# Two of fourteen large block products written out plainly, and the planner of sums, loads and tile places rewritten around them

## The reference, cut to what matters

```python
# x: (32, 128, 2048), all float32
def _L0(x, weight, bias, A, B, scale, id7):        # weight: (2048, 2048), A: (8, 16, 2048)
    base  = einsum('bsi,oi->bso', x, weight) + bias
    low   = einsum('bsi,bri->bsr', x, A[id7])
    delta = einsum('bsr,bor->bso', low, B[id7])
    return base + scale[id7][:, None, None] * delta
def _L1(x, weight, id14):                           # weight: (16, 2048, 2048)
    return einsum('bij,bkj->bik', x, weight[id14])
x = x + _L0(x, ...)
x = x + _L1(x, ...)
```

## Time and profile before

| | |
|---|---|
| median of three runs | 2754.98 us |
| the profiled execution | 2748.32 us |
| its span | 2746.5 us |
| mean granted TensorE clock | 0.971 |
| PE busy | 94% |
| DVE busy | 80% |
| ACT busy | 51% |
| POOL busy | 28% |

### The profile page before, as it was taken

How to read it: one execution, slowest core, us unless ns; L and a number is a source line. 1 busy time by engine, 2 the same in 40 slices (tenths; PEclk the granted TensorE clock), 3 DMA queues, 4 the chain that set the end, 5 groups by cost and what they waited for, 6 DMA issues and landing times.

```text
span 2746.5 us, 35355 instructions
## 1 busy us (share of the span) xinstructions
PE 2590.8 (94%) x12154; PEld 2128.2 (77%) x12154; DVE 2197.3 (80%) x1990; ACT 1389.4 (51%) x1486; POOL 779.1 (28%) x646
## 2 busy tenths in 40 slices
PE   7988789999998979997999999999999999999999
PEld 5767677878876767786888888888878878878887
DVE  7778679998885879987788887777877867877865
ACT  3324233334433323335666675666666756656665
POOL 4234334433333344411032131320320401302402
PEclk9999899999999989998999999999999999999999
DMA  5886796664389656976768768778699998998996
GB/s 218 320 290 204 195 245 174 197 202 155 111 265 264 170 140 162 291 251 239 274 228 301 250 225 298 252 261 275 243 343 342 326 355 337 321 346 306 310 320 232
DMA packets 218323, 702.97 MB, mean 256 GB/s; under 512 B 23936, under 2 KB 32288, under 8 KB 218144
## 3 DMA queue, kind: packets, MB, share of 16 engines
q1 hardware_dynamic: 201728, 640.94, 64.8%
q0 software_dynamic: 16128, 58.73, 10.9%
q10 hardware_dynamic: 288, 1.05, 0.1%
HBM read 675.45 MB, written 92.27 MB: 280 GB/s over the span
## 4 chain that ended last, share of the span: by engine, by line
PE 67%; DMA 13%; DVE 10%; issue 5%; POOL 2%; SPq 2%; ACT 1%; DVEq 0%; POOLq 0%; ACTq 0%
PE acc L1203 15%; PE acc L1204 15%; PE acc L1205 15%; PE acc L1120 7%; PE acc L1121 7%; PE acc L1122 7%; DMA wb<-w 5%; DMA xb<-x 4%; DVE tx L1075 2%; DVE ws L1075 2%; DMA xb<-x_sums 2%; DMA x_sums<-xb 1%; DVE acc L1064 1%; PE acc L1159 1%; DVE xb L980 1%
## 5 line engine op out<-in xcount | busy, mean ns | idle before, releaser
L1075 DVE TENSOR_TENSOR ws<-wb,ws 128x1024 fp32r<-128x1024 f32 x964 | 1244.5, 1318 | 322.9 <-ACT ws L906 310.1
L906 ACT CAST ws<-wb 128x1024 fp32r<-128x1024 f32 x964 | 985.7, 1050 | 793.0 <-PE acc L1205 422.7
L1203 PE MATMUL acc<-ws,ops 128*128 128x512 f32 (+1 forms) x2048 | 804.9, 393 | 33.8 <-DVE lows L1018 18.6
L1204 PE MATMUL acc<-ws,ops 128*128 128x512 f32 (+1 forms) x2048 | 801.5, 391 | 0.0
L1205 PE MATMUL acc<-ws,ops 128*128 128x512 f32 (+1 forms) x2048 | 800.8, 391 | 0.0
L1120 PE MATMUL acc<-tx,ws 128*128 128x512 f32 x1568 | 629.2, 401 | 112.9 <-DVE tx L1075 99.6
L815 POOL TENSOR_TENSOR wb<-wb,eye_s 128x128 f32<-128x128 f32 x384 | 318.6, 860 | 1201.9 <-DMA wb<-w 1201.7
L1121 PE MATMUL acc<-tx,ws 128*128 128x512 f32 x1568 | 624.5, 398 | 0.0
L1122 PE MATMUL acc<-tx,ws 128*128 128x512 f32 x1568 | 623.1, 397 | 0.0
L906 ACT CAST tx<-xb 128x1024 fp32r<-128x1024 f32 x196 | 205.9, 1051 | 538.3 <-PE acc L1122 268.9
L1203 PEld LDWEIGHTS acc<-ws,ops 128*128 128x128 f32 x2048 | 387.2, 189 | 115.9 <-DVE lows L1018 20.0
(11 more groups left out here) (66 smaller groups left out, 1115.8 us busy)
## 6 DMA issues: line engine op xcount, KB each, us to landing
wb<-w SPq DMA_DIRECT2D x832, 512.0 KB, 8.6
xb<-x SPq DMA_DIRECT2D x78, 512.0 KB, 7.0
y<-acc SPq DMA_DIRECT2D x32, 1024.0 KB, 6.7
xb<-x POOLq DMA_DIRECT2D x64, 512.0 KB, 9.2
out<-ost SPq DMA_DIRECT2D x128, 256.0 KB, 7.4
xst<-xt SPq DMA_DIRECT2D x60, 512.0 KB, 7.2
ystage<-y SPq DMA_DIRECT2D x60, 512.0 KB, 11.2
wb<-w_sums SPq DMA_DIRECT2D x48, 512.0 KB, 8.5
```

The lines of the kernel that those rows point to most:

```text
L906: eng.copy(hi, src).then_inc(s_hi, 1)
L1075: eng.tensor_tensor(lo, src, hi, ALU.subtract).then_inc(s_lo, 1)
L1203: eng.matmul(dst, yh, wh, start=begin, stop=False)
L1204: eng.matmul(dst, yh, wl, start=False, stop=False)
```

## The change

1. Outer products 0 and 1 (PLAIN) are computed by the class `Eight`: eight steps, all from unsummed tiles, no inner sums. Pairs of steps add up in the same PSUM bank, so that only every second step is evicted, and a split x tile (T) serves two steps (`new_t`), so that four steps have T splits. The other twelve products keep the seven steps (`Seven`). The stage has 100 steps instead of 98.
2. The weight sums of n = 2 to 5 are all made in advance by POOL (m1 to m4, for each of 8 halves p): four loads, four sums, and four stores to w_sums for each p. DVE's 16 "made" sums and all 48 accumulating weight DMAs are gone. Loads for n = 2 to 5 come from w_sums alone.
3. Places of x tiles follow need: the role that the next product needs first (b11) takes the place that is left first (step 3), then b12 (4), b22 (5), b21 (6).
4. `beside` has a second wait where DVE evicts the named step: POOL's inner sum also waits for the DVE task that stands just before the eviction of that step. s4 now goes through `beside` too, and s4 and s3 are planned with both halves in one step (t_of(s0 + 2), t_of(s0 + 3)): their first halves 8 to 11 us later than before, their second halves within 3 us of where they were.
5. Keys of t3 and t2 move later (t3 from s0 - 2 to s0 - 1), the accumulating x DMAs from +9 to +10.5, the saves of x sums from +16 to +22 after their load's key.

```diff
+class Eight:
+
+    t = ("b11", "b21", "b11", "b21", "b12", "b22", "b12", "b22")
+    w = ("a11", "a12", "a21", "a22", "a11", "a12", "a21", "a22")
+    blk = (None, 0, None, 2, None, 1, None, 3)
+    new_t = (0, 1, 4, 5)
+    fresh = (0, 2, 4, 6)
...
+    x_need = ("b11", "b21", "b12", "b22")
+    x_done = (("b11", 0), ("b21", 1), ("b12", 4), ("b22", 5))
+    w_need = ("a11", "a12", "a21", "a22")
+    w_done = (("a11", 4), ("a12", 5), ("a21", 6), ("a22", 7))
...
+class Seven:
...
+    x_need = ("b11", "b12", "b22", "b21")
+    x_done = (("b11", 3), ("b12", 4), ("b22", 5), ("b21", 6))
+    w_need = ("a21", "a22", "a11", "a12")
+    w_done = (("a21", 3), ("a11", 4), ("a12", 5), ("a22", 6))
...
+PLAIN = (0, 1)
+FORM = [Eight if q in PLAIN else Seven for q in range(NG * K)]
+STEPS = [(q, i) for q in range(NG * K) for i in range(len(FORM[q].t))]
...
-    def made_key(d, p):
-        return (18.0 + 9.0 * p, 32.0 + 15.0 * p)[d]
+    def made_key(p):
+        return MADE_FROM + MADE_EVERY * p
...
+            key = t_of(s) + (24 * h - 48) * MM + (3.2 if FORM[q] is Seven and (i, h) == (4, 0) else 0.25)
...
+    for p in range(8):
+        for i in range(4):
+            loads.append((made_key(p) - 12.0 + 0.1 * i, "made", (p, i)))
+        for i, after in ((1, 3.0), (0, 6.0), (2, 9.0), (3, 12.0)):
+            loads.append((made_key(p) + after, "keep", (p, i)))
...
-        if n in W_ADDED:
-            for role in W_ROLE:
-                for h in range(2):
-                    adds.append((lo_key("W", s0 - K + W_FREE[role], h) + 9.0, "wacc", (q, role, h)))
-        for h in range(2):
-            adds.append((past(s0 - 2 + h, 0.3) if q else -8.5 + 4.0 * h, "s1", (q, h)))
-            adds.append((past(s0 + h, 0.3) if q else lo_key("W", 0, h) + 8.0, "s2", (q, h)))
-            adds.append((past(s0 + 1 + h, 3.0 if h == 0 else 2.9), "s4", (q, h)))
-            adds.append((past(s0 + 2 + h, 0.3), "s3", (q, h)))
...
+        if FORM[q] is Eight:
+            continue
+        for h in range(2):
+            adds.append((t_of(s0 - 2 + h) + 0.3, "s1", (q, h)))
+            adds.append((t_of(s0 + h) + 0.3, "s2", (q, h)))
+            adds.append((t_of(s0 + 2) + 0.3 + 2.5 * h, "s4", (q, h)))
+            adds.append((t_of(s0 + 3) + 0.3 + 2.5 * h, "s3", (q, h)))
+        for c in range(2):
+            sums.append((t_of(s0 - 1) + 6.0 + 0.1 * c, "t3", (q, c)))
+            sums.append((t_of(s0 - 1) + 8.3 if c == 0 else t_of(s0) + 6.5, "t2", (q, c)))
+            sums.append((t_of(s0) + 8.0 + 0.1 * c, "t4", (q, c)))
+            sums.append((t_of(s0 + 1) + 8.0 + 0.1 * c, "t1", (q, c)))
...
+    for p in range(8):
+        for i, kind in enumerate(("m1", "m2", "m3", "m4")):
+            adds.append((made_key(p) + 3.0 * i, kind, (p,)))
...
+        before_ev = {}
+        for n, (_, what, _, index) in enumerate(vector_tasks):
+            if what == "ev" and index[1] == 0 and n:
+                _, was, k, old = vector_tasks[n - 1]
+                if was == "lo":
+                    before_ev[index[0]] = (s_lo, k + 1)
+                elif was == "ev":
+                    before_ev[index[0]] = (s_ev, ev_no[old])
+                elif (was, *old) in sum_no:
+                    before_ev[index[0]] = (s_sum, sum_no[(was, *old)])
...
+                if p >= 2:
+                    made_kept(eng, p - 2, i)
+                    eng.wait_ge(s_pool, pool_no["m4", p - 2])
...
             def beside(eng, s):
 
-                if s >= 0:
-                    eng.wait_ge(s_mm, at["W", s, 3] + 1)
+                if s in before_ev:
+                    eng.wait_ge(*before_ev[s])
+                eng.wait_ge(s_mm, at["W", s, 3] + 1)
```

More of the change, by code:

```diff
@@ L58 @@
 HOME = {"Y": (0, 0), "Z": (0, 1), "X": (1, 0), "Q": (1, 1)}
[L59 to L73, removed]
@@ L74 @@
-WS = [slots_of(("a11", "a12", "a21", "a22"), W_NEXT, q) for q in range(NG * K)]
+MADE_OF = ((1, 0), (1, 1), (0, 0), (0, 1))
+MADE_AS = (2, 0, 1, 3)
+MADE_FROM = 10.0
+MADE_EVERY = 18.0
+class Eight:
[4 more added lines that the diff above has]
+    fresh = (0, 2, 4, 6)
+    turn = (0, 2, 4, 6)
+    first = (1, 3, 5, 7)
+    last = {0: 1, 2: 3, 1: 5, 3: 7}
+    x_need = ("b11", "b21", "b12", "b22")
+    x_done = (("b11", 0), ("b21", 1), ("b12", 4), ("b22", 5))
+    w_need = ("a11", "a12", "a21", "a22")
+    w_done = (("a11", 4), ("a12", 5), ("a21", 6), ("a22", 7))
@@ new lines @@
+class Seven:
+    t = ("b11", "b21", "b11", "b11", "b12", "b22", "b21")
+    w = ("a11", "a12", "a11", "a21", "a11", "a12", "a22")
+    blk = (0, 0, 1, 3, 3, 1, 2)
+    new_t = (0, 1, 2, 3, 4, 5, 6)
+    fresh = (0, 1, 3)
+    turn = (0, 1, 2, 3, 4, 5, 6)
+    first = (0, 2, 3, 6)
+    last = {0: 1, 1: 5, 3: 4, 2: 6}
+    x_need = ("b11", "b12", "b22", "b21")
+    x_done = (("b11", 3), ("b12", 4), ("b22", 5), ("b21", 6))
+    w_need = ("a21", "a22", "a11", "a12")
+    w_done = (("a21", 3), ("a11", 4), ("a12", 5), ("a22", 6))
@@ L208, in program @@
                 if q == 0:
-                    key = -30.0 + {"a11": 1.0, "a21": 4.5, "a22": 8.0, "a12": 14.0}[role] + 1.2 * h
+                    key = -30.0 + {"a11": 1.0, "a12": 4.0, "a21": 10.0, "a22": 13.0}[role] + 1.2 * h
                 else:
-                    key = lo_key("W", s0 - K + W_FREE[role], h) + 1.5
+                    key = lo_key("W", W_FREED[q][role][1], h) + 1.5
                 loads.append((key, "w", (q, role, h)))
[L213 to L217, removed]
+    for p in range(8):
[3 more added lines that the diff above has]
+            loads.append((made_key(p) + after, "keep", (p, i)))
     tile_no = [None] * NRAW
@@ L292, in program @@
     fast, slow = [], []
-    for s in range(NSTEP):
-        n, i = s // K % K, s % K
-        for ot in range(4):
-            (fast if n in (0, 2) and i in FIRST else slow).append((ev_key(s, ot), s, ot))
+    for s, (q, i) in enumerate(STEPS):
+        if evicts(s):
+            for ot in range(4):
+                (fast if q % K in (0, 2) and i in FORM[q].first else slow).append((ev_key(s, ot), s, ot))
     fast.sort()
@@ L996, in _ @@
                         eng.tensor_tensor(q, x, q, ALU.add).then_inc(s_sum, 1)
-                    continue
-                if what == "made":
-                    d, p = index
-                    made_loaded(eng, d, p)
-                    one, other = made_tile(d, p, 0), made_tile(d, p, 1)
-                    eng.tensor_tensor(other, one, other, ALU.subtract).then_inc(s_sum, 1)
                     continue
```

307 lines of the change are left out of this document (169 added, 138 removed).

## The result

The changed kernel took 2622.78 us (median of four runs, 2619.82 to 2624.97) against 2749.96 us for the kernel before on the same chip: a ratio of 0.9539, with a 95% interval of 0.9507 to 0.9570. That is 127 us, 4.6% faster. The forecast was 2650 us with a range of 2612 to 2702, so sign and range held, and the gain was 27 us more than forecast. A second set of runs of the same kernel gave 2623.42 us, ratio 0.9548 (0.9523 to 0.9574).

A forecast was written before the change was run, and what follows sets the result against it. First-stage stalls and slow matmuls, 163 us over 10.88 us steps, were the winnable bound. Start 12.0 + steps 1100.0 + residues 5, 16, 7, 15 + second stage 1504.6 + 1.8 around gave 2649, said as 2650 us; range 2612 to 2702.

The forecast's parts named there:

- the residues: Stalls forecast to remain over the step floor in the first stage: 5, 16, 7 and 15 us, bounds 5 to 118.
- three releasers: Behind DVE in the first stage: late x tiles, DVE's own load with POOL collisions, and b21, whose place is left last.
- Products 0 and 1: First two products, 46.9 us over the floor: eight steps leave 5 us, between 0 and 25, with DMA the doubtful cover.
- Rival A: DMA at mean rates bounds the first 186 us, delaying made sums and x loads: 20 to 25 us more, 2672; chance 0.13.
- Products 2, 3, 9 and 10: Stalls of 71.2 us: fewer accumulating DMAs and earlier b11 leave 16 us, between 0 and 40.
- I leave 4 us for each: In products 2, 3, 9 and 10, b21 is late next and its store holds t4: 16 us in all.
- Products 4, 11 and 12: Stalls of 22.7 us: POOL's new wait leaves 2 to 4 collisions with DVE instead of 8; 7 us remain.
- Products 6 and 13: Stalls of 22.5 us: only collisions go, b21's load is neither earlier nor lighter; 15 us remain, between 5 and 30.
- B: DVE and b21 stay the bound: products 4, 6, 11, 12, 13 keep their stalls, four more get 6 us: 2697; chance 0.17.
- E: No change: the wait shifts from b11 to b22, t3 stalls DVE in products 2, 3, 9, 10: 2728 or 2743; chance 0.03.
- D: Slower: POOL, DVE and ACT lock in a ring of waits, delaying each of 96 inner halves; 2804 at 1.6 us; chance 0.04.
- C: Nearly all first-stage stalls go, residues of 10 us in all: 2617 us; chance 0.08.

## Why the prediction was right, and where it was off

**The bound.** Right: nearly all of the gain is in the first stage, its steps cost 10.88 us, and stalls and slow matmuls went together. Its end was forecast near 1143 us and is at 1119.6. These 23.4 us, in the residues, are most of the error of 27; the rest is rounding, 1.2 us in the second stage and the 2.2 us between the profiled execution and the median. What the list of three releasers lacked is a fourth: DVE's t3 and t2 behind the stores of x sums, 47.7 us, with PE's 10.7 us at the end of product 2.

**Products 0 and 1.** I left 5 us, and 3.7 stand, all in product 0. The cover held, but closely: the DMA share from 90 us to the start of product 2 is over 1.

```profile
90.00:150.00 60.00, 60.00 (x266) 49.70 (x265) 38.53 (x22) 21.09 (x23) 41.93 (x19) 1.00 1.03 377
150.00:190.00 40.00, 40.00 (x179) 33.11 (x178) 27.00 (x20) 8.48 (x9) 19.40 (x14) 1.00 1.04 362
```

The count of 175 to 191 us of transfers in 184 was about right: in the two products the DMA engines were busy for some 177 us and moved 64.5 MB, where I had counted 67. Rival A did not come: the last of the made sums' stores was issued at 176.5 us, 13 us before product 2, and nothing on PE stood for them. The rate here is 362 to 377 GB/s for a hundred microseconds, and so under the 410 GB/s of 10 us, a short row that was no rate to plan with. The Trainium skill gives about 358 as the limit (DMA: Bandwidth & Descriptors, Specifications); this trace is 1 to 5% above it, so the measurement decides, but for a long stretch the page's figure was the nearer one. What I did not work out is the other form: seven steps with the made sums on POOL would have cost 59 us over the floor in these two products and 8 in the next, not 47. Eight steps are worth some 40 us in this kernel, with their price of 21.8 us on PE paid.

**Products 2, 3, 9 and 10.** I left 16 us and 1.0 stands. The step that failed is "I leave 4 us for each": I put b21 next in line behind b11 and expected its store to hold t4. PE waits for b21 in none of the four. Products 3 and 10 are at the floor as soon as the accumulating weight DMAs go, with nothing else changed; product 2 took more than that: it had 7.4 us left in the kernel before without the accumulations, 7.8 in the changed kernel without eight steps, and 6.8 in the one without the wait for DVE. Within this step I also gave b11's earlier place too much: with the later t3 and t2 it is worth 8 us in the kernel before, and taken out of the changed one 11, and the latter by a store and not by a late load. The accumulations are worth 82.

**Products 4, 11 and 12.** I left 7 us; under 0.1 stand. The cause that I gave, DVE's collisions with POOL, is half of it; the other half is that DVE came late into the product. Without the accumulations the steps are whole with no wait for DVE; with the wait they are nearly whole with the accumulations. I took one cure for the only one. With DVE on time PE's signal puts POOL's sum beside the eviction by itself; with DVE behind, only the wait does.

**Products 6 and 13.** I left 15 us and 14.9 stand, but for partly wrong reasons. Of product 13's 10.9 us some 6 are matmuls of the second stage that run within it (3.9 us in the third step, 2.1 in the seventh), which I had counted as stall before and after alike. b21 is late, as I said, and its place is not what binds: with the two stores behind its load, and the place as it was, PE no longer waits in either product's first two steps.

**The rivals.** B and E fell: no 13.6 us step is left and DVE never waited for b22's load over 0.4 us. D fell: POOL's two largest new waits for DVE come to 95 us, and PE stood 9.1 us for DVE in all. DVE and POOL still meet: 6.77 us for two sums that take 2.35 alone, and DVE full for 76 us in the run with one product in eight steps. The lock between the two that the Trainium skill tells of (SBUF — State Buffer, Who interferes with whom) agrees with that. C, nearly all stalls gone, was the nearest case: 2617 us. I gave it 0.08, so the range held, but I had its middle in the wrong place.

## What to carry to other kernels

Look at how much one queue must bring, at the trace's own pace for that kind of transfer, before crediting an earlier place or start: here freeing places early halved ACT's waits for x tiles and was worth 8 us, a tenth of taking 48 of the queue's 112 transfers away (82 us). A long wait on an engine is no time that can be won until the next tile due behind it has been looked at. A form with more matmuls can be the faster one where it frees the engine that feeds them: two steps more on PE (21.8 us) took some 64 us of stalls away. And where two cures may each be enough for a stall, apply each alone to the kernel before and take each out of the changed one; either trace by itself names only one.

## What I had not expected of the hardware

The accumulating weight DMAs cost far more than their bytes: 48 of 512 KB, 25 MB in a stage of 266 MB, were worth 82 us, while POOL's waits for them were worth a few us at most. In product 3 the DMA share was 0.78 with them, at 207 GB/s over 94.0 us, and 0.67 without, at 189 GB/s over 76.3 us: the DMA engines were never full in either, and without them everything came in time. And DMA ran at a share of 1.03 to 1.04 for 100 us beside PE at full rate and clock, without one matmul waiting. One more: DVE and POOL can hold each other in a bad rhythm. In product 4 of the kernel before each step cost DVE 4.4 us of meetings, which kept it behind, which brought about the next ones.
